# A two-layer expert feed-forward beside differential attention: the second layer in three f32r products, with low halves made on GpSimd

## What is computed

```python
# attention: 16 sub-heads of 8, values in 8 heads of 16
q, k = rope(xn @ Wq.T), rope(xn @ Wk.T)
probs = softmax(q @ k.T)                       # per sub-head, 1024 x 1024
diff = probs[even] - lam * probs[odd]          # lam from four small vectors
attn = rms_normalise(diff @ v) * (1 - LAMBDA_INIT)
# feed-forward: a router on the mean token picks 3 of 8 zones per batch
z = sum(w[e] * (gelu(xn @ Wa[e]) @ Wb[e]) for e in top3)
out = x + attn @ Wo.T + xn + z
```

## Time and profile before

| | |
|---|---|
| runs, median (lowest to highest) | 479.25 us (478.18 to 480.07) |
| the profiled execution's own time | 479.25 us |
| its span in the trace | 477.5 us |
| TensorE busy, products | 440.6 us, 92% |
| VectorE busy | 390.8 us, 82% |
| ScalarE busy | 305.9 us, 64% |
| GpSimd busy | 57.2 us, 12% |
| mean granted clock of TensorE | 0.968 of full speed |

### The profile page before, as it was taken

How to read it: one execution, slowest core, us unless ns; L and a number is a source line. 1 busy time by engine, 2 the same in 40 slices (tenths; PEclk the granted TensorE clock), 3 DMA queues, 4 the chain that set the end, 5 groups by cost and what they waited for, 6 DMA issues and landing times.

```text
span 477.5 us, 6978 instructions
## 1 busy us (share of the span) xinstructions
PE 440.6 (92%) x2575; PEld 185.7 (39%) x2575; DVE 390.8 (82%) x742; ACT 305.9 (64%) x376; POOL 57.2 (12%) x68
## 2 busy tenths in 40 slices
PE   8396699999999989999999999999999999999987
PEld 6385444444444423333333333333333333233235
DVE  2778498988898959999989998989999999995125
ACT  1431132233222358889888988897988988899972
POOL 4157651100200000000000000000000000000000
PEclk9697699999999979999999999999999999999999
DMA  8507874110000130001002020000000000000002
GB/s 301 205 1 228 306 278 157 45 30 17 1 3 0 45 134 2 2 17 74 3 0 86 7 89 1 3 0 3 1 3 1 1 1 3 1 2 3 0 2 88
DMA packets 12036, 25.62 MB, mean 54 GB/s; under 512 B 1250, under 2 KB 5986, under 8 KB 11874
## 3 DMA queue, kind: packets, MB, share of 16 engines
q1 hardware_dynamic: 11570, 22.37, 13.6%
q10 hardware_dynamic: 432, 2.81, 1.6%
HBM read 15.48 MB, written 9.44 MB: 52 GB/s over the span
## 4 chain that ended last, share of the span: by engine, by line
PE 62%; DVE 13%; ACT 9%; issue 8%; DMA 4%; SPq 2%; POOL 1%; ACTq 0%; DVEq 0%; POOLq 0%
PE ps L957 17%; PE ps L927 15%; PE ps L892 10%; ACT E L516 8%; PE ps L950 8%; DVE part_max L677 8%; DMA X<-in_x 3%; PE ps L811 2%; PE ps L812 2%; PE ps L813 2%; DMA q_scr<-ropeL 1%; PE ps L1023 1%; SPq L300 1%; PE ps L1032 1%; PE ps L1026 1%
## 5 line engine op out<-in xcount | busy, mean ns | idle before, releaser
L677 DVE TENSOR_REDUCE part_max<-ps 128x1 f32<-128x512 f32 x512 | 319.1, 679 | 33.0 <-PE ps L927 32.1
L516 ACT ACTIVATE E<-ps 128x1024 f32<-128x1024 f32 x256 | 245.7, 1027 | 38.2 <-PE ps L950 37.2
L957 PE MATMUL ps<-E,Vg 128*32 128x512 f32 x1024 | 138.1, 612 | 1.6 <-ACT E L516 1.1
L927 PE MATMUL ps<-K,Q 32*128 32x512 f32 x384 | 109.1, 477 | 2.0 <-DVE part_max L677 1.7
L950 PE MATMUL ps<-Q,K 32*128 32x512 f32 x384 | 89.8, 486 | 6.6 <-ACT E L516 4.5
L927 PEld LDWEIGHTS ps<-K,Q 32*128 32x128 f32 x384 | 46.8, 184 | 91.6 <-DVE part_max L677 84.4
L495 ACT ACTIVATE h<-ps 128x512 f32<-128x512 f32 x48 | 28.7, 597 | 78.2 <-PE ps L813 78.0
L892 PE MATMUL ps<-h,wb_f 128*128 128x512 f32 x96 | 53.8, 642 | 0.0
L950 PEld LDWEIGHTS ps<-Q,K 32*128 32x128 f32 x384 | 37.0, 184 | 38.4 <-ACT E L516 34.2
L438 POOL TENSOR_TENSOR U<-AT,rsum 128x256 f32<-128x256 f32 x15 | 9.3, 621 | 307.6 <-DVE rsum L732 307.6
L811 PE MATMUL ps<-xnH,waH 128*128 128x512 f32 x48 | 36.4, 758 | 0.0
(11 more groups left out here) (139 smaller groups left out, 321.2 us busy)
## 6 DMA issues: line engine op xcount, KB each, us to landing
k_scr<-ropeH SPq DMA_DIRECT2D x6, 512.0 KB, 5.3
K<-k_scr SPq DMA_DIRECT2D x6, 512.0 KB, 4.8
Q<-q_scr SPq DMA_DIRECT2D x6, 512.0 KB, 5.7
tab<-in_tables ACTq DMA_DIRECT2D x1, 2048.0 KB, 11.0
q_scr<-ropeL SPq DMA_DIRECT2D x4, 512.0 KB, 5.7
q_scr<-ropeH SPq DMA_DIRECT2D x4, 512.0 KB, 6.7
wa_raw<-in_wa SPq DMA_DIRECT2D x6, 256.0 KB, 2.8
wb_raw<-in_wb SPq DMA_DIRECT2D x6, 256.0 KB, 3.0
```

The costliest lines, as they stand in the source:

```text
L516: nc.scalar.activation(E[:, par, 2 * jj:2 * jj + 2, :].rearrange("p j t -> p (j t)"), ps[:, 2 * jj:2 * jj + 2, :].rearrange("p j t -> p (j ...
L677: nc.vector.tensor_reduce(part_max[:, tile // FC % 2, j * FC + tile % FC, sh:sh + 1], ps[:, SLOT_BANK[quad_slot(t) + k], :], AX.X, ALU.max ...
L927: mm(ps[:, SLOT_BANK[x], :], Qs[g % KQ_BUFS][strip(j), tile % TB * P:(tile % TB + 1) * P], Ks[g % KQ_BUFS][strip(j), sh * BANK:(sh + 1) * ...
L957: last = mm(ps[QUAD * j:QUAD * (j + 1), B_PV, :], Vg[:, par, st, j // 2, :], E[:, s % 2, k, :], start=(st == 0), stop=(st == TB - 1), skip ...
```

## The change

The second layer becomes three f32r products. ScalarE writes gelu twice, as f32 (h, two buffers) and rounded to f32r (hH); GpSimd subtracts them (hL, `h_low`). Wb's scaled f32 form is split too: wbH by ScalarE (`wb_zone_high`), wbL by GpSimd (`wb_zone_low`). Rope pieces 6 and 7 on GpSimd move behind h_low(3) and h_low(7), and wa_zone(e) behind the third unit of zone e - 1.

A half's negated maxima are split before the transpose, on GpSimd (`half_negate`); one transpose then gives 32 rows, and VectorE copies them once (`max_out`). The transpose stands two quads later. GpSimd's list in attention follows the steps for that. VectorE's lambda operations move to step 116, and the first two heads_sum two steps later.

Unit 44 uses banks 4 and 5 alone for slots, units 45 to 47 banks 4, 5 and 2. Scores 0 and 1 of step 0 go out ahead of unit 46; scores 2 and 3 follow inside step 0. The last sum is copied between the first two exponentials. `rope_piece` holds the unchanged body of the loop at L398, `shares_of_rows` that of L435, and `lambdas` that of L699 to L715.

```diff
+HF_BUFS = 2
...
 def quad_slot(t):
 
-    return 4 * t + max(0, (t - 1) // 8)
+    return 4 * t + max(0, (t - 3) // 8)
 
 
 def half_slot(hx):
 
-    return min(33 * hx + 36, SLOTS - 1)
+    return min(33 * hx + 44, SLOTS - 1)
...
-    return (4, 5, 2, 3) if n < 22 else (4, 5, 3, 0) if n < 26 else (4, 5, 0, 1)
+    return (4, 5, 2, 3) if n < 22 else (4, 5, 3, 0) if n < 26 else (4, 5, 0, 1) if n < 44 else (4, 5) if n < 45 else (4, 5, 2)
...
-        extra = (t % 8 == 0 and t > 0) + (t == QUADS - 1)
+        extra = (t % 8 == 2 and t > 2) + (t == QUADS - 1)
...
+SUM_2_SLOT = next(x for x in range(last_lead_slot((2,), 22) + 1, SLOTS) if SLOT_BANK[x] == 2)
...
-HEADS_AT = (MAX_STEPS + 2, MAX_STEPS + 3, ALL_STEPS - 3)
+HEADS_AT = (MAX_STEPS + 4, MAX_STEPS + 5, ALL_STEPS - 3)
...
-                for part, row in ((maxH, MAX_ROW), (maxL, MAX_ROW + 1)):
+                for part, row in ((max_hl[0:16], MAX_ROW), (max_hl[16:32], MAX_ROW + 1)):
...
+            def wb_zone_low(e):
+                par = e % 2
+                pool.wait_ge(wbh_done, e + 1)
+                nc.gpsimd.tensor_tensor(wbL[:, par, :], wb_f[:, par, :], wbH[:, par, :], ALU.subtract).then_inc(wb_split, 1)
+
+            def half_negate(hx):
+
+                pool.wait_ge(neg_f_done, hx + 1)
+                if hx >= 2:
+                    pool.sem_inc(pool_waited, 1)
+                    pool.wait_ge(half_made, hx - 1)
+                nc.gpsimd.tensor_copy(neg_max[:, hx % 2, 0:16], neg_f[:, hx % 2, :]).then_inc(neg_high, 1)
+                pool.wait_ge(neg_high, hx + 1)
+                nc.gpsimd.tensor_tensor(neg_max[:, hx % 2, 16:32], neg_f[:, hx % 2, :], neg_max[:, hx % 2, 0:16],
+                                        ALU.subtract).then_inc(neg_done, 1)
+
+            def h_low(n):
+                pool.wait_ge(gelu_done, n + 1)
+                pool.sem_inc(pool_waited, 1)
+                pool.wait_ge(hs_free, n + 1)
+                nc.gpsimd.tensor_tensor(hL[:, n % H_BUFS, :], h[:, n % HF_BUFS, :], hH[:, n % H_BUFS, :],
+                                        ALU.subtract).then_inc(hl_done, 1)
+
+            for m in range(4):
+                rope_piece(m)
+            for m in range(4, 6):
+                rope_piece(m)
+                wa_zone(m - 4)
+            wb_zone_low(0)
+            for n in range(UNITS):
+                h_low(n)
+                if n in (3, 7):
+                    rope_piece(6 + n // FC)
+                e = n // UZ + 1
+                if e >= 2 and n % UZ == 2 and e < PICKS:
+                    wa_zone(e)
+                if n % UZ == 5 and e < PICKS:
+                    wb_zone_low(e)
+                for t, k in lead_slots(n - 3) if n >= 3 else ():
+                    if t % TB == TB - 1 and k == GJ - 1:
+                        half_negate(t // TB)
...
+            for s in range(ALL_STEPS):
+                for t, k in max_slots(s - 1) if s else ():
+                    if t % TB == TB - 1 and k == GJ - 1:
+                        half_negate(t // TB)
+                if s % TB == 3 and s > TB:
+                    shares_of_rows(s // TB - 1)
...
             def gelu(n):
                 act.wait_ge(g1_done, n + 1)
+                if n >= HF_BUFS:
+                    act.wait_ge(hl_done, n + 1 - HF_BUFS)
+                nc.scalar.activation(h[:, n % HF_BUFS, :], ps[:, 6 + n % 2, :], ACT.Gelu_apprx_tanh).then_inc(h_done, 1)
                 act.wait_ge(hs_free, n + 1)
-                nc.scalar.activation(h[:, n % H_BUFS, :], ps[:, 6 + n % 2, :], ACT.Gelu_apprx_tanh).then_inc(gelu_done, 1)
+                nc.scalar.activation(hH[:, n % H_BUFS, :], ps[:, 6 + n % 2, :], ACT.Gelu_apprx_tanh).then_inc(gelu_done, 1)
+
+            def wb_zone_high(e):
+                act.wait_ge(wb_done, e + 1)
+                nc.scalar.activation(wbH[:, e % 2, :], wb_f[:, e % 2, :], ACT.Copy).then_inc(wbh_done, 1)
...
+            wb_zone_high(0)
             for n in range(UNITS):
                 gelu(n)
+                if n % UZ == 5 and n // UZ + 1 < PICKS:
+                    wb_zone_high(n // UZ + 1)
...
             nc.scalar.activation(lt[:, 6:7], eps[:], ACT.Exp).then_inc(warm, 1)
-            sums_copy(CHUNKS - 1)
...
+            def exp_pair(n, jj):
+                act.wait_ge(st_done[jj], 2 * n + 2)
+                act.wait_ge(e_free, n + 1)
...
+            def exps(n):
+                exp_pair(n, 0)
+                exp_pair(n, 1)
...
-            exps(0, 0)
+            exp_pair(0, 0)
+            sums_copy(CHUNKS - 1)
+            exp_pair(0, 1)
             for s in range(ALL_STEPS):
                 if s + 1 < ALL_STEPS:
-                    exps(s + 1, (s + 1) % 2)
+                    exps(s + 1)
...
                     dve.wait_ge(slot_read, quad_slot(t) + 4)
-                    nc.vector.tensor_reduce(neg_max[:, hx % 2, :], part_max[:, hx % 2, :, :], AX.X, ALU.max,
-                                            negate=True).then_inc(neg_done, 1)
-                if t % TB == 0 and t:
-                    max_split(t // TB - 1)
+                    if hx >= 2:
+                        dve.wait_ge(neg_done, hx - 1)
+                    nc.vector.tensor_reduce(neg_f[:, hx % 2, :], part_max[:, hx % 2, :, :], AX.X, ALU.max,
+                                            negate=True).then_inc(neg_f_done, 1)
+                if t % TB == 2 and t > 2:
+                    max_out(t // TB - 1)
                 if t == QUADS - 1:
-                    max_split(2 * GROUPS - 1)
-
-            def max_split(hx):
-                bank = SLOT_BANK[half_slot(hx)]
+                    max_out(2 * GROUPS - 1)
+
+            def max_out(hx):
                 dve.wait_ge(half_made, hx + 1)
-                nc.vector.tensor_copy(maxH[:, hx % 2, :], ps[0:16, bank, 0:P]).then_inc(maxh_done, 1)
-                dve.wait_ge(maxh_done, hx + 1)
-                nc.vector.tensor_tensor(maxL[:, hx % 2, :], ps[0:16, bank, 0:P], maxH[:, hx % 2, :],
-                                        ALU.subtract).then_inc(slot_read, 1)
-
...
+                nc.vector.tensor_copy(max_hl[:, hx % 2, :], ps[0:32, SLOT_BANK[half_slot(hx)], 0:P]).then_inc(slot_read, 1)
+
+            def lambdas():
+                dve.wait_ge(lam_exp, 1)
...
+                if s == MAX_STEPS:
+                    lambdas()
...
-                mm(ps[:, chunk(n), :], wb_f[:, n // UZ % 2, f * P:(f + 1) * P], h[:, n % H_BUFS, :], start=False, stop=end,
+                par, f = n // UZ % 2, slice(f * P, (f + 1) * P)
+                mm(ps[:, chunk(n), :], wbH[:, par, f], hH[:, n % H_BUFS, :], start=False, stop=False, skip_group_check=True)
+                mm(ps[:, chunk(n), :], wbL[:, par, f], hH[:, n % H_BUFS, :], start=False, stop=False, skip_group_check=True)
+                mm(ps[:, chunk(n), :], wbH[:, par, f], hL[:, n % H_BUFS, :], start=False, stop=end,
                    skip_group_check=True).then_inc(hs_free, 1)
...
+                    if x == SUM_2_SLOT:
+                        pe.sem_inc(pe_waited, 1)
+                        pe.wait_ge(z_out, 3)
...
-                nc.tensor.transpose(ps[0:16, SLOT_BANK[x], 0:P], neg_max[:, hx % 2, :], ident).then_inc(half_made, 1)
+                nc.tensor.transpose(ps[0:32, SLOT_BANK[x], 0:P], neg_max[:, hx % 2, :].bitcast(F32), ident).then_inc(half_made, 1)
...
-                if k == GJ - 1 and t % TB == 0 and t:
+                if k == GJ - 1 and t % TB == 2 and t > 2:
                     half_transpose(t // TB - 1)
...
-                        pe.wait_ge(slot_read, last_lead_slot((c,)) + 1)
+                        pe.wait_ge(slot_read, last_lead_slot((c,), n) + 1)
                         start_sum(c)
+                if n == UNITS - 2:
+
+                    pe.wait_ge(qmax_in, 32)
+                    pe.wait_ge(slot_read, last_lead_slot((0, 1)) + 1)
+                    pe.sem_inc(e_free, 2)
+                    score(0, 0)
+                    score(0, 1)
...
                 if n % UZ == 0:
-                    pe.wait_ge(wb_done, n // UZ + 1)
-                pe.wait_ge(gelu_done, n + 1)
+                    pe.wait_ge(wb_split, n // UZ + 1)
+                pe.wait_ge(hl_done, n + 1)
                 second(n)
-            pe.wait_ge(qmax_in, 32)
-            pe.wait_ge(slot_read, last_lead_slot((0, 1)) + 1)
-            pe.sem_inc(e_free, 2)
-            score(0, 0)
-            score(0, 1)
-            pe.wait_ge(z_out, CHUNKS)
-            score(0, 2)
-            score(0, 3)
...
+                if s == 0:
+                    pe.wait_ge(slot_read, last_lead_slot((2,)) + 1)
+                    pe.sem_inc(pe_waited, 1)
+                    pe.wait_ge(z_out, CHUNKS)
+                    score(0, 2)
+                    score(0, 3)
```

(27 more changed lines are left out.)

38 lines of the change are left out of this document (10 added, 28 removed).

## The result

The changed kernel takes 475.23 us in the median of five runs (475.17 to 475.57), beside 478.78 for the kernel before: a ratio of 0.9926, 95% interval 0.9908 to 0.9943. It is faster by 3.6 us where 10.9 were forecast (468.4 from 479.25), and inside the upper end of the range, 475.5, by 0.3. The profiled execution's span went from 477.5 to 473.4.

A forecast was written before the change was run, and what follows sets the result against it. TensorE was taken to bound feed-forward, three nearly full engines attention. Feed-forward 7.5, transition 2.0 and attention 2.0, less a stall of 0.6, give 10.9 off 479.25: 468.3, say 468.4 us, range 463 to 475.5.

The forecast's parts named there:

- Second layer: Feed-forward: one f32 product of 0.96 becomes three f32r products totalling 0.70, saving 0.26 us per unit, 2.19 to 1.93.
- the 2.4 stays: Last 32 feed-forward units: the 2.4 us above ordinary unit time, for starts of sums and transposes of halves, remains.
- GpSimd in the start: First feed-forward units: GpSimd runs late, so second(8) starts no earlier than 80.4 and only 0.6 us is won by unit 12.
- VectorE beside GpSimd: Feed-forward units 12 to 44: four wb_f operations slowed beside GpSimd cost 1.8 us more, 1.4 of it reaching TensorE.
- The short ring: Last feed-forward units: three banks for slots cost nothing; two banks for three slots can cost 0 to 0.5 us.
- The transition: Feed-forward to attention: early scores and exponentials remove VectorE's idle time, taken as 2.0 us won, bounds 0.5 and 3.5.
- The rival on the clock: Start, 62 to 82 us: TensorE's waits for GpSimd make the clock drop; time 471.4 to 474, chance 0.18.
- Attention: Twelve halves in attention: VectorE loses maxL and a handshake, 3.6 us in all; between 0 and 3.6, 2.0 taken as won.
- The row of maxima of half 14: Attention, near step 111: scores of step 112 wait for the later maxima, a stall of 0.6 us once, bounds 0 and 2.
- The tail: End of the kernel: heads two steps later cost nothing, since ScalarE has the same work.
- The rival in which VectorE takes the pace: Whole kernel: wb_f waits fully, four-bank ring runs dry; feed-forward wins 4.5, transition 1, attention nothing; 474.3 us, chance 0.14.
- Its form at the far end: The rival in which VectorE takes the pace, with a two-microsecond stall: 475.5 us, the slow end of the range.

The follow-up runs named there:

- the second trace: The changed kernel itself, with nothing altered, run and traced once more on the same chip: 474.54 us, ratio 0.9917.
- The later rope pieces: Changed kernel with rope pieces 6 and 7 behind h_low(7) and h_low(15), and the first sum copied two gelus later: 472.72 us, ratio 0.987.
- The two runs with another ring: Changed kernel, units 44 to 47: old banks 4, 5, 0, 1, first scores after the last unit, 473.99 us; or wider, up to 4, 5, 2, 7, 473.46 us.
- fillers: Changed kernel with three extra 512-column products into bank 6 after the seconds of units 44 to 47 and twice more in step 0: 475.33 us.
- The half reductions: Changed kernel with every reduction of a slot in attention reading 256 of its 512 columns: 469.0 us.
- both mendings: Changed kernel with wider slot banks at the end of feed-forward and rope pieces 6 and 7 behind h_low(7) and h_low(15): 468.83 us, ratio 0.9818.

## Why the prediction was right, and where it was wrong

Direction and most mechanisms held; the size did not, 3.6 us for 10.9, and so the forecast is wrong. By its steps:

- **Second layer.** This is the main failed step. The term was mis-sized: "Saved: 0.26 per unit" measured 0.16, since the f32 product costs 0.86 and not 0.96. What failed is the reading of the earlier trace rows, where all the time from the second's record to L811 was put to the product. Of it, 0.10 us belong to the place behind the slots, and stay. Over 31 units that is about 3 us. Then "the 2.4 stays", for starts of sums and transposes of halves, did not hold either: the time above ordinary units is 2.5 before and 3.3 after from second(12) to second(43), and units with a transpose now take 2.66 to 2.79. Against these 3.8 stand 1.4 that had been set aside for wb_f and were hardly needed. So feed-forward fell short by about 2.5 up to second(43), with 0.2 of it ahead of second(12). ScalarE and GpSimd, priced at 1.20 per unit and 14.0 per eight units, stayed beside, as forecast: GpSimd is busy for 12.8 to 14.1 us in eight units of 16.8 to 17.3.
- **GpSimd in the start.** Right in kind and number: second(8), forecast at 80.4, came at 80.0 (79.4 in the second trace); h_low takes 1.29; second(12) won 0.4 of the 0.6 forecast. The later rope pieces show that the lateness was the cause. Right as well that it hides the lambda move.
- **VectorE beside GpSimd.** The operation on wb_f (count, then ns of the shortest, the middle and the longest):

```profile
L688 DVE TENSOR_SCALAR wb_f<-wb_raw,wbc x6: 601/692/979, 52.1 to 137.7; 128x512 f32<-128x512 f32 x6
```

  Mostly between the two prices, 0.69 in the middle and up to 0.98, never the 0.47 of an idle GpSimd. The four of units 12 to 44 or just ahead took 0.60 to 0.76, some 0.7 us above the idle price together, where 1.8 was forecast. The Trainium skill's rule (SBUF — State Buffer, Who interferes with whom) agrees in kind; its bound of a whole GpSimd operation, 1.28 more, was not reached. The operations were taken to let 1.4 through to TensorE. Units 11, 19 and 27 start 2.03 after the one before, and units 20 and 35, near two of the operations, 2.16: at most 0.4 came through.
- **The short ring.** "They cost nothing", with 0 to 0.5 for two banks: for its size this failed most. It measured 1.3 in unit 44 (3.29 against 2.02), and the milestones lose 1.5 from second(43) to second(47). The two runs with another ring take 7.7 and 7.9 us over these four units, the changed kernel 9.1. The step argued from VectorE's rate on three banks in attention. There TensorE has scores and values to issue between slots; here three slots stand in a row in front of a second, and each wait for a bank holds the second and what follows it.
- **The transition.** "Taken as 2.0": 1.0 measured, from second(47) to the first copy. The scores went out early, as forecast, but the clock fell 7.5 us sooner than before, and VectorE's idle time ahead of its slots there is 1.61 and 1.30, not under 1. All six traces with the short ring and no fillers show the fall between 159.4 and 164.3; with the old or the wider ring it comes at 166.2 or later or not at all. So the fall goes with the ring; by which of its waits is not shown. The rival on the clock had the right mechanism in the wrong place: the clock held in the start (1.00 from 60 to 84), where the holes were, and fell at the end.
- **Attention.** "Between 0 and 3.6 I take 2.0": it was 0, 270.5 us before and after. A high share of VectorE's time was taken as a share in the limit. The half reductions give its exchange rate, 8%, by which, as an estimate, 3.6 us are worth 0.3. maxL did go, with no measurable effect.
- **The row of maxima of half 14.** "A stall of 0.6 once": none. The transpose starts at 415.87, the two issues at 417.47 and end at 418.57, and scores of step 112 go out at 420.84, together with a slot that had waited for VectorE. From the transpose to the issues' end it is 2.7, as read, without the 0.3 that was to go; landing took at most 2.3. But 5.0 us were available and not 4.2.
- **The tail** was priced at nothing, and is 0: 15.4 us from the last copy to the end in both.
- **The rival in which VectorE takes the pace** gave 474.3, the nearest number, with 4.5 won in feed-forward, 1 in the transition and nothing in attention. That is close to what the milestones show, but by luck: its reason, that every wb_f waits fully and the ring of four banks runs dry at each, did not occur. Its form at the far end, with a stall of 2.0, adds up to 475.75 (479.25 - 5.5 + 2.0) and not to 475.5; the measured time is inside by either.

The sum again, against the 10.9: 2.5 short by second(43), 1.9 between there and second(47) (1.5 lost, and 0.3 more that was forecast), 1.0 in the transition, 1.5 in attention. With rounding these are the 6.8 us by which the span, which won 4.1, fell short.

## What to carry to other kernels

Price a product by the distance between products of its own kind, or double it; a gap where the shape of the products changes belongs to neither. Where slots pass between two engines that are both nearly full, count banks against the burst that is issued in a row, not against the mean rate. When a newly loaded engine is late at the start of a stage, move its independent work to where it has slack, before judging the scheme by its total.

## What the runs showed of the hardware that was not expected

TensorE's granted clock made a larger loss of small waits. In the changed kernel it went from 1.00 to 0.50 just before 164, after stretches in which TensorE was busy for 3.66 of 4 us (156 to 160), 1.68 of 2 (160 to 162) and 1.85 of 2 (162 to 164). Yet it had kept 1.00 through 3.14 of 4 at 76 to 80, and with both mendings it kept 1.00 through 0.84 of 2 at 162 to 164. So its fall is not told by such shares alone.

In the changed kernel it stayed low to about 174. With fillers the transition was 1.4 us shorter, and with both mendings 2.9, but there TensorE also had other waits. Between executions of the same kernel, the one with both mendings, 1.9 us separate two groups with different mean clocks. Full clock could not be bought at a profit with fillers of 0.7 us.

The other is the 0.10 us behind the slots. It is paid by the first product of 128 rows that follows products of 32 rows: 0.53 where the same f32 instruction otherwise takes 0.43, and 0.34 where the f32r product takes 0.23.
